# A fused FFN kernel on one core: the order of the lists on VectorE and ScalarE around td, the down projection's LoRA rows and the sum of y

## The reference

```python
gate = lora_add(x @ W_gate.T, x, A_gate, B_gate)       # F = 1376 features, rank 16, adapter by itok_B_2_6
up   = lora_add(x @ W_up.T,   x, A_up,   B_up)
act  = jax.nn.silu(gate) * up
down = lora_add(act @ W_down.T, act, A_down, B_down)
x = x + down @ sign(L0_ffn_weight).T + L0_ffn_bias
Bx  = jnp.einsum('bni,bri->bnr', x, B[itok_B_4_50])    # rank 16, adapter by itok_B_4_50
low = jnp.einsum('bnr,bor->bno', Bx, A[itok_B_4_50])
x = x + ffn(low)                                       # W, bias and eight LoRA adapters, weighted
```

## Time and profile before

| what | us |
|---|---|
| median of 3 runs | 991.69 (991.62 to 991.92) |
| the profiled execution, its own time | 993.31 |
| its span in the trace | 991.5 |
| PE busy in it | 969.8 |
| DVE busy | 729.2 |
| ACT busy | 387.7 |
| POOL busy | 382.2 |

### The profile page before, as it was taken

The page is one execution under the profiler, slowest core; times in us unless marked ns, Lnnn a source line. Parts: engine busy times, 40 slices in busy tenths (PEclk is TensorE's granted clock), DMA queues, the critical chain, the costliest instruction groups (busy, mean ns, idle before and its releaser), DMA issues.

```text
span 991.5 us, 19299 instructions
## 1 busy us (share of the span) xinstructions
PE 969.8 (98%) x5371; PEld 860.0 (87%) x5371; DVE 729.2 (74%) x1594; ACT 387.7 (39%) x669; POOL 382.2 (39%) x528
## 2 busy tenths in 40 slices
PE   9989999999999999999999999999999999999997
PEld 6778988999888888988888898899888988888896
DVE  6775777777777777777777777777777777877775
ACT  5753343333334333334343333334333333343332
POOL 1323434344443443444344333444434443334232
PEclk9999999999999999999999999999999999999999
DMA  9934444454445344444444454445445544544431
GB/s 354 361 97 107 112 109 113 129 139 118 123 115 130 102 126 132 138 109 120 124 120 111 125 140 115 120 122 129 109 118 132 129 116 114 128 113 117 128 103 43
DMA packets 155982, 128.64 MB, mean 130 GB/s; under 512 B 51648, under 2 KB 132800, under 8 KB 155840
## 3 DMA queue, kind: packets, MB, share of 16 engines
q1 hardware_dynamic: 145296, 94.37, 34.6%
q0 software_dynamic: 10672, 34.09, 12.4%
HBM read 86.45 MB, written 11.01 MB: 98 GB/s over the span
## 4 chain that ended last, share of the span: by engine, by line
SPq 46%; DMA 15%; issue 14%; DVE 12%; PE 8%; ACT 4%; DVEq 0%; ACTq 0%; POOL 0%; POOLq 0%
SPq L347 20%; DMA landed<-act_sb 8%; SPq L317 5%; SPq L325 5%; PE gu_ps L1052 4%; DMA a_raw<-in_atab 4%; SPq L309 4%; SPq L322 4%; SPq L314 4%; SPq L306 3%; PE y_ps L1116 2%; DVE act_sb L839 2%; DMA c_table<-rows_out 2%; DVE act_sb L778 2%; ACT actT_sb L502 2%
## 5 line engine op out<-in xcount | busy, mean ns | idle before, releaser
L1116 PE MATMUL y_ps<-down_sb,actT_sb 128*128 128x288 f32 x2112 | 296.5, 295 | 3.3 <-DVE x_sb L833 2.7
L1116 PEld LDWEIGHTS y_ps<-down_sb,actT_sb 128*128 128x128 f32 x2112 | 288.5, 188 | 11.3 <-issue 5.3
L1052 PE MATMUL gu_ps<-wg_sb,xT_sb 128*128 128x512 f32 (+1 forms) x1152 | 274.4, 387 | 0.2 <-POOL xT_sb L445 0.2
L1052 PE MATMUL gu_ps<-wu_sb,xT_sb 128*128 128x512 f32 (+1 forms) x1152 | 259.8, 370 | 0.0
L1052 PEld LDWEIGHTS gu_ps<-wg_sb,xT_sb 128*128 128x128 f32 x1152 | 211.3, 188 | 36.4 <-POOL xT_sb L445 0.4
L1052 PEld LDWEIGHTS gu_ps<-wu_sb,xT_sb 128*128 128x128 f32 x1152 | 206.6, 189 | 31.9
L731 DVE TENSOR_TENSOR b_sb<-b_raw,b_sb 64x1024 fp32r<-64x1024 f32 (+2 forms) x128 | 126.4, 988 | 73.3 <-ACT b_sb L502 57.6
L502 ACT CAST b_sb<-b_raw 64x1024 fp32r<-64x1024 f32 (+2 forms) x128 | 104.7, 818 | 101.6 <-DMA b_raw<-in_b1tab 100.8
L402 POOL DMA_INDIRECT b_raw<-in_btab,now x96 | 100.0, 1042 | 79.4 <-POOL now L416 74.6
L416 POOL TENSOR_TENSOR now<-now 128x1 int32<-128x1 int32 x160 | 49.2, 307 | 208.2 <-DVE b_sb L731 142.1
L502 ACT CAST actT_sb<-landed 128x512 fp32r<-128x512 f32 (+1 forms) x95 | 55.5, 585 | 175.7 <-DMA landed<-act_sb 163.5
(11 more groups left out here) (171 smaller groups left out, 941.8 us busy)
## 6 DMA issues: line engine op xcount, KB each, us to landing
landed<-act_sb SPq DMA_DIRECT2D x376, 64.0 KB, 2.1
ad_raw<-in_adtab SPq DMA_DIRECT2D x128, 88.0 KB
xT_raw<-in_xT SPq DMA_DIRECT2D x32, 256.0 KB
a_raw<-in_atab SPq DMA_DIRECT2D x128, 64.0 KB
x_sb<-in_x SPq DMA_DIRECT2D x31, 256.0 KB, 3.5
out_x<-x_sb SPq DMA_DIRECT2D x31, 256.0 KB
landed<-act_sb SPq DMA_DIRECT2D x128, 48.0 KB
b_raw<-in_b1tab SPq DMA_DIRECT2D x124, 32.0 KB
```

What stands on the lines that cost most here:

```text
L1052: last = nc.tensor.matmul(o, w, m, start=start and n == 0, stop=stop and n == len(terms) - 1, skip_group_check=not check)
L1116: last = nc.tensor.matmul(y_ps[half][:, 0:MH], actT_sb[:, ACTT_SLOT[c] + n, a, :], down_sb[:, blk, b, half * MH:(half + 1) * MH], start=c ...
```

## The change

No work is added or taken away; the lists are reordered.

- In DVE's list: `split_td` and `split_ad` come before `split_actT(g, 0)`, and `add_y(prev)` comes before `split_actT(g, 1)`.
- In ACT's list: `split_ad` and `split_td` come before `split_actT(g, 0)`; `silu(g, 2)` comes before `split_actT(g, 1)`, and in step 0 the split of the next xT as well.
- In PE's list: `down_lora(prev)` stands behind two quarters of up 2 instead of one.
- In step 0, on DVE and ACT: t is turned and split ahead of the B rows (on ACT behind the B rows of chunk 1), and `split_up(2, ...)` stands between the B rows of chunk 1 and chunk 2 (on ACT right behind t) instead of ahead of the step.

```diff
@@ ACT step
+                if prev is None:
+                    split_t(g)
+                    split_up(2, range(KC))
                 split_b(g, 2)
...
-                split_t(g)
+                    split_t(g)
...
+                split_ad(g)
+                if prev is not None:
+                    split_td(prev)
                 split_actT(g, 0)
-                split_ad(g)
-                if prev is not None:
-                    split_td(prev)
-                split_actT(g, 1)
                 silu(g, 2)
+                if prev is not None:
+                    split_actT(g, 1)
                 if nxt is not None:
                     split_xT(nxt)
+                if prev is None:
+                    split_actT(g, 1)
@@ DVE step
+                if prev is None:
+                    own_t(g)
+                    turn_t(g)
+                    split_t(g)
                 split_b(g, 1)
+                if prev is None:
+                    split_up(2, range(KC))
...
-                split_actT(g, 0)
                 if prev is not None:
                     split_td(prev)
                 split_ad(g)
+                split_actT(g, 0)
+                if prev is not None:
+                    add_y(prev)
                 split_actT(g, 1)
                 if prev is not None:
-                    add_y(prev)
                     turn_x1(prev)
@@ PE step
-                up(g, 2, range(0, 1))
+                up(g, 2, range(0, 2))
                 if prev is not None:
                     down_lora(prev)
-                up(g, 2, range(1, KC))
+                up(g, 2, range(2, KC))
```

More of the change, by code:

```diff
@@ L717, in _ @@
             rows_stored(act)
-            split_up(2, range(KC))
             step(0, None, None, 1)
@@ L881, in step @@
                 split_b(g, 2)
-                own_t(g)
-                turn_t(g)
+                if prev is not None:
+                    own_t(g)
+                    turn_t(g)
                 if pp is not None:
```

## The result

The changed kernel has a median of 977.42 us (976.85 to 981.73, 4 runs), the kernel before 991.65 us (990.53 to 991.92, 4 runs) beside it. The ratio is 0.9868 with an interval of 0.9839 to 0.9897: 14.2 us less. The profiled executions have spans of 975.3 and 991.5 us, 16.2 us apart; the one of the kernel before is 1.7 us over its median, the changed one 0.3 under, which is the 2.0 us between the two differences.

A forecast was written before the change was run, and what follows sets the result against it. The prediction took x1's turn-to-turn cycle through other engines, longer than PE's 28.17 us, to bound the loop. Loop 7.0 plus front 6.0 made 13.0 us, from 991.69 to 978.7 us, range 972.5 to 986.5.

The forecast's parts named there:

- the front: Steps 0 to 2: 8.9 us of waits and slow clock go, PE gives back 2.9, leaving 6.0 us won.
- its own signs: Changed profile: no t wait or half clock, no td waits from step 3, steps of 28.3 to 28.5 us.
- The cycle as the loop's bound: Loop: x1's turn in one step sets the next through SP and DVE, 28.70 us in step 7 against PE's 28.17.
- The order on the port: Loop: POOL's bias sum and DVE's subtractions exclude each other on the memory port, giving a cycle of 28.24 to 28.44.
- both cases of it: POOL's sum goes between ad and chunk 0, cycle 28.24 us, or last, behind chunk 0's subtraction, cycle 28.44 us.
- The loop's term: 28 steps of the loop fall from 28.63 to 28.38 us each, winning 7.0 of the 12.8 us lost.
- rival 1: Loop: PE is the bound, the cycle gets under 28.17 and all 12.8 us go: 972.9 us; chance 0.17.
- td's waits at nothing: Loop: td comes 1.3 us early for `down_lora`, so PE's waits for td are costed at nothing.
- 1.7 us for the half clock in step 0: Step 0: slow matmuls behind the 3.39 us wait for t cost 1.7 us more, counted as won in the front.
- rival 4: Loop: x's load becomes the bound; landing 0.7 us later makes the cycle 29.10 and the time 998.9 us; chance 0.07.
- Rival 2: Loop: the cycle stays as long as before, x landing some 0.2 us later; only the front wins: 985.7 us; chance 0.18.
- rival 3: Front gives nearly nothing, B rows' gather or chunk 0's landing holding the first down product; only 1.7 us count: 983.0; chance 0.08.

The follow-up runs named there:

- the second execution: The changed kernel profiled once more without an edit, beside two other kernels on the same chip: 977.24 us, ratio 0.9861.
- the second execution of the kernel before: The kernel before, unchanged, run again for a second trace: 990.39 us (one run).
- the same without the first sum: The kernel before with POOL's sum of x and the first bias cut to 8 columns instead of 512: 987.67 us, ratio 0.9961.

## Why the prediction was right

The forecast was 978.7, the result 977.42; a gain of 13.0 us was forecast and 14.2 measured. The parts of the sum are less close than the sum, and that is partly luck. In the spans, from which the terms were read, the gain is 16.2 us, 3.2 more than forecast: the loop 4.0 more, the front 0.25 more, and 1.05 lost at the end. The medians are 2.0 us closer together, because the profiled execution of the kernel before was slower than its median.

By its own signs the prediction was right in the front and wrong about the steps of the loop. The wait for t and the half clock are gone, waits for td are gone from step 3 on, and chunk 0's subtraction is stretched. But steps of 28.3 to 28.5 us and waits of 0.1 to 0.4 us for the second add in most steps did not come: 15 of the 28 steps take 28.17 us, which the prediction had named as a sign of being wrong.

**The cycle as the loop's bound** holds. It predicts that what shortens the chain from x1's turn to x1's turn shortens the step even where PE waits little. Two experiments changed one link each: the adds behind chunk 1 lengthened the mean step by 0.36 us, and x loaded late by 2.52. That the way back from x1's turn to td's low half runs beside PE and not through it shows in its length: 23.46 to 23.80 us in the changed kernel's loop and 23.46 to 24.15 with x late, where a step takes 2.5 us more. In the changed kernel the cycle has come down to PE's own time, so that both bind.

**The order on the port** holds, both cases of it. 17 of 32 subtractions of chunk 0 take 1.64 or 1.65 us in the changed profile, where 4 of 32 took over 1.6 before. In these steps POOL goes first. In the second execution there are 22. Where DVE goes first it looks like the seam one step ahead of the one shown above:

```profile
497.78 0.29 DVE L736 TENSOR_TENSOR tdT_sb<-tdT_raw,tdT_sb 128x128 fp32r<-128x128 f32 x1 [0.37 <-ACT tdT_sb L502]
...
498.79 0.55 DVE L736 TENSOR_TENSOR actT_sb<-landed,actT_sb 128x384 fp32r<-128x384 f32 x1
500.59 0.45 DVE L837 TENSOR_TENSOR x_sb<-x_sb,y_ps 128x288 f32<-128x288 f32 x1 [1.25 <-POOL x_sb L437]
...
501.87 0.70 DVE L844 STREAM_TRANSPOSE act_sb<-x_sb 128x512 f32<-128x512 f32 x1
```

```profile
499.08 1.41 POOL L437 TENSOR_TENSOR x_sb<-x_sb,bias_sb 128x512 f32<-128x512 f32 x1 [4.11 <-DMA x_sb<-in_x]
```

From td's low half to the end of x1's turn it is 502.57 - 497.78 = 4.79 us here, and 530.64 - 526.10 = 4.54 with POOL first. The forecast had 282.14 - 277.40 = 4.74 and 281.94 - 277.40 = 4.54. The rule of the Trainium skill that was cited ("SBUF — State Buffer", section "SBUF: two separate sides") agrees with both seams: ad's subtraction, chunk 0's and POOL's sum go one after the other, in either order.

**The loop's term was mis-sized**: 7.0 us forecast, 11.0 measured. The prediction took 28.38, "in the upper half" of 28.24 to 28.44. Two things were off. First, the working from x1's turn to td's low half: it had 277.40 - 253.70 = 23.70 us. In the changed kernel it is 526.10 - 502.57 = 23.53 in one step and 23.59 in the step before. The low half of a ends 19.95 and 20.01 us after the turn of x1 instead of 20.15. The value of step 7 was one of a scatter: over the loop it is 19.91 to 20.48 before (mean 20.09) and 19.89 to 20.23 after (mean 20.03). So the two cases give 28.07 and 28.38 at these seams, and 28.13 and 28.40 in the mean over the loop, not 28.24 and 28.44.

Second, how often each case comes. The forecast leaned on the one with DVE first, because POOL's sum began late in step 7, 25.07 us after x1's turn; in the trace of the kernel before it begins earlier in 22 of 28 steps, at 24.48 in the median. In the changed kernel POOL goes first in 16 of the 28 cycles, DVE in 11. The mean over all of them is 28.23, and that is PE's mean step. A cycle under 28.17 does not shorten PE's step but pays back a long one: DVE gets ahead of PE in steps with 28.07, and a cycle of 28.42 can then cost PE nothing (it ends at 756.30, and PE's step around it, from 729.61, takes 28.17). Where several long ones come together PE does wait, as in the two steps up to the seam just shown, 28.22 and 28.46. 15 of the 28 steps take 28.17 us, and in the second execution 23. The mean of 28.23 is thus nearly rival 1 (PE is the bound), and taking out POOL's sum, which brings exactly 28.17, shows how little is missing. The lesson of both is the same: the forecast read its durations from one step, where 28 were on the trace.

**td's waits at nothing** holds: none is left in the list of the first execution, and one of 0.7 us in that of the second. The prediction put this down to DVE's order and PE's move together. Undone singly, DVE's order brings back 5.2 us of waits for td in the trace, PE's move 2.5.

**The front** was forecast at 6.0 us and is 6.25. t's low half ends at 63.88 (forecast 63.5, since the mask began 0.5 us later than assumed) and chunk 1's turn at 74.00 (forecast 74.0). Against the 8.9 us that the waits and slow stretches cost before, PE gives back 8.9 - 6.25 = 2.65 us, from the end of step 0 (0.65 us) to step 2; the forecast had 2.9 us in steps 1 and 2. Step 2 takes 29.31 us, 1.1 over PE's own time, and step 3 28.60. What was counted as fixed is not: 1.7 us for the half clock in step 0. The second execution of the kernel before has the wait without it, and its step 0 takes 24.3 us instead of 25.6, so where the stretch came it cost 1.3 us and not 1.7. The gain in the front is then 141.78 - 135.90 = 5.9 us between the two second executions.

**The end of the program** was not charged, a term that the sum lacks. It costs 1.05 us, about the wait of 1.18 us for x1 at 958.38. The move of PE's `down_lora` was costed by what it covers in the loop, and the adds ahead of chunk 1 by the loop's chain; undoing either alone shortens this wait, to 0.51 and 0.70 us. In the last step the chain from td over the adds to x1 ends in a product that PE reaches at once, so what is a spare 1.2 us at the seam shown above is a wait there.

**The rivals.** The late x of rival 4 is a real mechanism, with 28.84 as the point from which it turns the sign, but x did not land late: only the run that moved its load shows it. Rival 1 (PE is the bound) came nearest in the loop: 11.0 of its 12.8 us. Rival 2 (a cycle as long as before) and rival 3 (a front that gives nothing) did not come about. Rival 3's mechanism shows in the run with the step 0 edits alone, where chunk 0's landing and the down LoRA rows behind it hold the first down product for 1.80 us, and PE waits 3.07 us for td in step 2.

## What to carry to other kernels

When the bound engine's own step is shorter than the measured one and its waits are small and scattered, look for a ring through other engines' lists (here x1's turn, SP's list, a, td, the adds, x1's turn), and order the list that closes it by what the ring needs, with the pieces that wait for a landing last. Taking away one wait at the head of a pipeline moves PE forward, but not the engine that feeds it: the gain is what both move. Look separately at the last step, where an operation moved later has nothing to hide behind. And read a duration that is to be multiplied by 28 from all 28 steps.

## What the runs showed of the hardware

The clock after a given wait is not fixed. Behind nearly the same wait of 3.38 or 3.39 us in step 0, PE ran at 1.2 GHz for 3.4 us in the kernel before, for 6.8 us in the same without the first sum, and not at all in the second execution of the kernel before or with the loop's lists alone. Waits of 2.1 and 1.95 us in step 2 were followed by such a stretch, a wait of 3.07 us was not: the window behind it, in the kernel with the step 0 edits alone, reads 1.00.

```profile
133.60:140.00 6.40, 6.39 (x38) 5.82 (x39) 5.36 (x8) 1.74 (x3) 2.68 (x4) 1.00 0.15 39
```

The Trainium skill ("TensorE: Matmul & The Clock Gate", "What's actually happening") says of a kernel's start that how much runs at the lower clock varies from run to run. These runs show the same behind a wait in the middle, with 0, 3.4 and 6.8 us. So such a stretch is a price with a chance, and the price is under the 1.7 us of the sum: step 0 of the kernel before took 25.6 us with 3.4 us of it, 24.3 without, and 26.7 with 6.8 us in the kernel without the first sum. It may be part of why the kernel before varies more (987.43 to 999.08 over all its runs, the changed one 976.02 to 981.73); that was not tested, and the sets ran on different chips.
